# Moving half of a three-term sum from VectorE to GpSimd in an edge pass of a graph network

## The chip, the cores and the metric

The kernel runs on one core of one Trainium2 chip. The metric is the device time of one execution in microseconds (us). The kernel before was timed three times: 6016.84, 6020.4 and 6021.12 us, median 6020.4. One further execution was recorded by the profiler.

## The reference, cut to what matters

The whole kernel applies four graph layers to 6250 nodes with 256 features. The change touches only the edge pass of layer 0. Its 106250 edges are sorted by destination. For each edge the reference computes

```
g0 = f0[edge_src]                      # 64 scalars of the source node
g1 = f1[edge_src]                      # 64 vectors of 3
y0 = edge_attr[:, 0]; y1 = edge_attr[:, 1:4]
m0a = wa * g0 * y0[:, None]
m0b = wb * einsum('eum,em->eu', g1, y1) / sqrt(3)      # a dot product of 3 terms
m1a = wc[:, :, None] * g0[:, :, None] * y1[:, None, :]
m1b = wd[:, :, None] * g1 * y0[:, None, None]
```

where wa, wb, wc and wd come from a small network on the ten further features of the edge. The messages (512 numbers an edge) are summed over the edges of each destination node. The dot product in m0b needs three products, which are formed one by one, and two additions. The change is about these two additions.

## The kernel before, in words

The edges lie in 880 steps of 128 edges, one edge in each partition. Four steps make a group q, and there are 220 groups (NQ). Each engine runs its own program, a loop over periods p = -3 to 221, and in each period every engine works on a group at a different depth of the pipeline. Order between the engines is kept by semaphores, written out by hand; there is no scheduler. In a wait such as `freed(act, s_v, 2 * q - 2)` the engine waits until the semaphore has reached the value, and values of zero or less are not waited for.

- **GpSimd** (L1421) gathers, for each step k, 128 rows of 256 numbers out of the table in HBM by an indirect DMA into one of 8 buffers of G. Before gather k it waits (s_y) until ScalarE has used up the buffer, that is until step k - 8 is done.
- **ScalarE** (`vectors`, L1442 and L1445) scales each gathered row by the four edge attributes: four activations a step. Seven of the message slots go to the tile zt, in one of three sets (z), and the three products of the dot product go to one of two sets t in the same tile. Its first activation of group q waits until the additions of group q - 2 have read set t (s_v). `silu` (L1430) forms the hidden layer of the edge network, once a group, between the second and third step.
- **TensorE** computes the edge weights into PSUM (pE, `edge_weights`, L1548), the hidden layer (pH, L1541), and scatters the messages: `scatter` (L1557) multiplies the 128 x 128 matrix `one` (which edge belongs to which node) with the 512 numbers of a step into pM, one of two PSUM buffers. The first scatter of a group waits for `pair` of that group.
- **VectorE** has the most to do. In period p it issues, in this order: `mark(p)` (L1482, builds `one` for group p out of the PSUM copy pI and relS), `add(p-2, 3)` (L1518, adds pM into the accumulator of a node tile), `dots(p)` (L1489 and L1491, the two additions of the dot product, both with two inputs in SBUF; the second waits for the first), `add(p-1, 0)`, `three(p, 1, 2)` (L1497, three slots times the edge weight), `add(p-1, 1)`, `three(p, 5, 3)` (L1497), `add(p-1, 2)`, `pair(p)` (L1503, the last two slots times their weights). The products read pE from PSUM and zt from SBUF, the adds read acc from SBUF and pM from PSUM.
- Every `add` waits for its scatter (s_m) and for the add before it (s_acc). Every 16 steps, that is once in four periods, `add(p-1, 0)` first loads 16 node numbers into VectorE's registers (L1509).
- **SyncE** loads the edge features and clears the accumulator.

Of the kernel before, what the change touches and what calls it, by code (L numbers as in the profile page):

```python
# [25 lines left out]
K = U2 * math.ceil((ET + math.ceil(N / P) - 1) / U2)  # L26
# [11 lines left out]
def build(nc, a, out):  # L38
# [5 lines left out]
    ALU = mybir.AluOpType  # L44
# [4 lines left out]
    def dram(name, shape, dt=F32):  # L49
        return nc.dram_tensor(name, shape, dt).ap()  # L50
# [55 lines left out]
    table = [dram(f"table{n}", [NP, w]) for n, w in enumerate((D, D + H1, D, D + H3))]  # L106
# [6 lines left out]
    with top:  # L113
# [6 lines left out]
        srcI = top.sb("srcI", [P, KP], I32)  # L120
# [35 lines left out]
        def freed(eng, sem, value):  # L156

            if not (type(value) is int and value <= 0):
                eng.wait_ge(sem, value)
# [577 lines left out]
        def tile(t, n):  # L737

            return t[:, ds(n, 1), :].rearrange("p a c -> p (a c)")
# [187 lines left out]
        with Stage() as st0:  # L927
# [5 lines left out]
            with Stage() as st:  # L933
# [4 lines left out]
                with Stage() as sx:  # L938
# [31 lines left out]
                    s_v, s_tk, s_nd, s_ndd, s_ndr, s_w1, s_w2 = (sx.sem(n) for n in ("s_v", "s_tk", "s_nd", "s_ndd", "s_ndr", "s_w1", "s_w2"))  # L970
# [385 lines left out]
            with Stage() as st:  # L1356
                acc = st.sb("acc0", [P, NT, 2 * D])
                with Stage() as se:
                    NQ, GS, NZ = K // 4, 8, 3
                    G = se.sb("G", [P, GS, D])  # L1360
# [12 lines left out]
                    pM = [se.ps(f"pM{j}", [P, 2 * D]) for j in range(2)]  # L1373
                    pI = se.ps("pI", [P, P])
                    s_w, s_z, s_c, s_i, s_y, s_v, s_p = (se.sem(n) for n in ("s_w", "s_z", "s_c", "s_i", "s_y", "s_v", "s_p"))
                    s_h, s_hs, s_e, s_one, s_m, s_acc = (se.sem(n) for n in ("s_h", "s_hs", "s_e", "s_one", "s_m", "s_acc"))
                    s_g = [se.sem(f"s_g{j}") for j in range(GS)]
                    s_a = [se.sem(f"s_a{j}") for j in range(2)]
                    CLEAR = 4
# [3 lines left out]
                    def z_of(q):  # L1383

                        return zt[:, q % NZ * 32:q % NZ * 32 + 32, :].rearrange("p (s b) c -> p s b c", s=4)

                    def t_of(q):
                        at = NZ * 32 + q % 2 * 12
                        return zt[:, at:at + 12, :].rearrange("p (s m) c -> p s m c", s=4)

                    def periods(do):
                        for p in range(-3, NQ + 2):
                            do(p)

                    with nc.Block() as block:
# [20 lines left out]

                        @block.gpsimd
                        def _(pool):
                            for k in range(K):
                                freed(pool, s_y, k - GS + 1)  # L1420
                                pool.indirect_dma_start(G[:, k % GS, :], None, table[0],  # L1421
                                                        bass.IndirectOffsetOnAxis(ap=srcI[:, k:k + 1], axis=0)).then_inc(s_g[k % GS], 16)

                        @block.scalar
                        def _(act):
                            def silu(q):
                                if 0 <= q < NQ:
                                    act.wait_ge(s_h, q + 1)
                                    freed(act, s_e, 4 * q - 4)
                                    nc.scalar.activation(hid[q % 2][:, :, :], pH[:, :, :], ACT.Silu, scale=1 / math.sqrt(NBAS)).then_inc(s_hs, 1)  # L1430

                            def vectors(q, s):
                                if 0 <= q < NQ:
                                    k = 4 * q + s
                                    act.wait_ge(s_g[k % GS], 16 * (k // GS) + 16)
                                    freed(act, s_m, k - 4 * NZ + 1)
                                    if s == 0:
                                        freed(act, s_v, 2 * q - 2)
                                    g = G[:, k % GS, :].rearrange("p (b c) -> p b c", c=MUL)
                                    zi = q % NZ * 32 + s * 8  # L1440
                                    ti = NZ * 32 + q % 2 * 12 + s * 3
                                    nc.scalar.activation(zt[:, zi:zi + 4, :], g, ACT.Copy, scale=a4S[:, 0, k:k + 1])  # L1442
                                    for m in range(3):
                                        to = slice(zi + 5 + m, ti + m + 1, ti - zi - 5)
                                        ins = nc.scalar.activation(zt[:, to, :], g[:, 0:m + 2:m + 1, :], ACT.Copy, scale=a4S[:, 1 + m, k:k + 1])  # L1445
                                    ins.then_inc(s_y, 1)

                            def period(p):
                                vectors(p + 1, 0)
                                vectors(p + 1, 1)  # L1450
                                silu(p + 2)
                                vectors(p + 1, 2)
                                vectors(p + 1, 3)
                            periods(period)

                        @block.vector
                        def _(dve):
# [26 lines left out]

                            def dots(q):
                                if 0 <= q < NQ:
                                    dve.wait_ge(s_y, 4 * q + 4)
                                    z, t = z_of(q), t_of(q)
                                    nc.vector.tensor_tensor(z[:, :, 4, :], t[:, :, 0, :], t[:, :, 1, :], ALU.add).then_inc(s_v, 1)  # L1489
                                    dve.wait_ge(s_v, 2 * q + 1)  # L1490
                                    nc.vector.tensor_tensor(z[:, :, 4, :], z[:, :, 4, :], t[:, :, 2, :], ALU.add).then_inc(s_v, 1)  # L1491

                            def three(q, b, w):
                                if 0 <= q < NQ:
                                    dve.wait_ge(s_e, 4 * q + 4)
                                    z = z_of(q)[:, :, b:b + 3, :]
                                    nc.vector.tensor_tensor(z, pE[q % 2][:, :, w, :].unsqueeze(2).broadcast_to([P, 4, 3, MUL]), z, ALU.mult)  # L1497

                            def pair(q):
                                if 0 <= q < NQ:  # L1500
                                    dve.wait_ge(s_v, 2 * q + 2)
                                    z = z_of(q)[:, :, 0:5:4, :]
                                    nc.vector.tensor_tensor(z, pE[q % 2][:, :, 0:2, :], z, ALU.mult).then_inc(s_p, 1)  # L1503

                            def add(q, s):
                                k = 4 * q + s
                                if 0 <= q < NQ:
                                    if k % 16 == 0:
                                        _, values = nc.values_load_multi_w_load_instructions(  # L1509
                                            nodeA[0:1, ds(k, 16)], engines=[dve.engine], min_val=0, max_val=NT - 1,  # L1510
                                            skip_runtime_bounds_check_because="the setup clamps every step's node to the node tiles")
                                        at.update(enumerate(values))
                                    if k % 2 == 0 and k // 2 in s_clear:
                                        dve.wait_ge(s_clear[k // 2], 16)
                                    dve.wait_ge(s_m, k + 1)
                                    freed(dve, s_acc, k)
                                    to = tile(acc, at[k % 16])
                                    nc.vector.tensor_tensor(to, to, pM[k % 2][:, :], ALU.add).then_inc(s_acc, 1)  # L1518

                            def period(p):  # L1520
                                mark(p)
                                add(p - 2, 3)
                                dots(p)
                                add(p - 1, 0)
                                three(p, 1, 2)
                                add(p - 1, 1)
                                three(p, 5, 3)
                                add(p - 1, 2)
                                pair(p)
# [252 lines left out]
        with Stage() as st3:  # L1782
# [22 lines left out]
            with Stage() as st:  # L1805
# [9 lines left out]
                s_w, s_c, s_at, s_t, s_tc, s_o, s_r, s_y, s_yb, s_l = (  # L1815
                    st.sem(n) for n in ("s_w", "s_c", "s_at", "s_t", "s_tc", "s_o", "s_r", "s_y", "s_yb", "s_l"))
                s_x = [st.sem(f"s_x{q}") for q in range(5)]
                s_v = [st.sem(f"s_v{j}") for j in range(4)]
# [90 lines left out]
            with Stage() as st:  # L1909
# [8 lines left out]
                s_l, s_h, s_t, s_tc, s_f, s_fc, s_o, s_r = (st.sem(n) for n in ("s_l", "s_h", "s_t", "s_tc", "s_f", "s_fc", "s_o", "s_r"))  # L1918
# [66 lines left out]
            with Stage() as st:  # L1985
                CH = NT // 5
                s_m, s_x, s_out = st.sem("s_m"), [st.sem(f"s_x{q}") for q in range(5)], st.sem("s_out")
# [50 lines left out]
```

## Time and profile before

| | |
|---|---|
| median of three runs | 6020.4 us |
| the profiled execution | 6016.6 us |
| its span (first to last instruction) | 6014.9 us |
| VectorE busy over the span | 4179.2 us (69%) |
| GpSimd busy over the span | 3617.6 us (60%) |
| ScalarE busy over the span | 2463.8 us (41%) |
| TensorE busy over the span | 4348.8 us (72%) |
| layer 0's edge pass | about 285 us to 1706 us of the span |

The shares of the whole span are means over stages with different limits, and for a change in one stage only the rows of that stage count. A row of a timeline gives the start, the length, the engine, the line, the operation and its tiles; neighbours of one kind are merged, with their number behind an x, and in brackets stands how long the engine sat idle before and what ended that. The records of two neighbouring VectorE instructions overlap by some 0.08 us, so the cost of one instruction in a full queue is the distance between two starts and not its own length.

### The profile page before, as it was taken

What the parts mean: (1) busy time and instruction counts of PE and PEld (TensorE: products, weight loads), DVE (VectorE), ACT (ScalarE), POOL (GpSimd) and SP (SyncE); (2) the same over time, 40 slices, a digit from 0 to 9 for tenths busy, and PEclk for the clock granted to TensorE, in tenths of its full rate; (3) what the DMA queues carried; (4) which work ended last, traced back from release to release, by engine and by line L of the source; (5) the groups of instructions that cost most, each with busy time, mean ns of one, the idle gap of its engine ahead of it and who ended that gap; (6) DMA issues with size and microseconds to landing.
All of it is one profiled execution on the core that took longest, in us unless ns stands there. A gap on an engine that the chain in (4) does not pass through costs nothing. (4 is left out here: it accounts for less than half of the span.)

```text
span 6014.9 us, 78255 instructions
## 1 busy us (share of the span) xinstructions
PE 4348.8 (72%) x17463; PEld 2676.3 (44%) x17463; DVE 4179.2 (69%) x9983; ACT 2463.8 (41%) x6920; POOL 3617.6 (60%) x4190
## 2 busy tenths in 40 slices
PE   2799999999995665566567777777856666666596
PEld 1544444444474444444343433344434444444385
DVE  5599999999975556555555555555657766776766
ACT  2498888988853333333320000000113333333343
POOL 3465555555526777777567777777357777775001
PEclk9899999999987777777777677777877777777898
DMA  6453333333335555555333333333235555553301
GB/s 166 162 160 98 98 98 98 97 99 97 98 106 148 140 143 145 141 141 144 110 98 105 105 106 105 105 105 105 95 106 147 148 144 146 147 147 106 100 0 44
DMA packets 468850, 699.69 MB, mean 116 GB/s; under 512 B 212924, under 2 KB 310800, under 8 KB 468262
## 3 DMA queue, kind: packets, MB, share of 16 engines
q0 software_dynamic: 171200, 474.81, 28.4%
q1 hardware_dynamic: 284336, 207.07, 11.9%
q10 hardware_dynamic: 12896, 13.11, 0.6%
q8 instruction: 157, 2.57, 0.2%
q14 instruction: 261, 2.14, 0.1%
HBM read 620.77 MB, written 70.10 MB: 115 GB/s over the span
## 5 line engine op out<-in xcount | busy, mean ns | idle before, releaser
L275 POOL DMA_INDIRECT G<-table,srcI x1760 | 1673.6, 951 | 582.7 <-issue 497.9
L544 PE MATMUL pS<-G,one 128*128 128x260 f32 (+1 forms) x3520 | 1203.6, 480 | 192.2 <-issue 96.2
L1421 POOL DMA_INDIRECT G<-table,srcI x880 | 830.1, 943 | 600.1 <-ACT zt L1445 545.3
L1557 PE MATMUL pM<-zt,one 128*128 128x512 f32 x1760 | 945.2, 618 | 113.3 <-DVE zt L1503 73.7
L477 ACT ACTIVATE acc<-pS x1760 | 691.7, 393 | 779.3 <-PE pS L544 519.5
L625 POOL DMA_INDIRECT G<-table,srcI x880 | 833.5, 947 | 280.9 <-issue 149.0
L661 PE MATMUL pM<-G,one 128*128 128x256 f32 x1760 | 790.5, 555 | 254.7 <-issue 132.5
L1445 ACT ACTIVATE zt<-G,a4S 128x128 f32<-128x128 f32 x2640 | 856.9, 390 | 0.0
L544 PEld LDWEIGHTS pS<-G,one 128*128 128x128 f32 x3520 | 593.0, 212 | 263.3 <-issue 210.1
L661 PEld LDWEIGHTS pM<-G,one 128*128 128x128 f32 x1760 | 374.0, 255 | 657.5 <-DVE one L634 515.3
L641 DVE TENSOR_TENSOR acc<-acc,pM 128x256 f32 x880 | 370.4, 421 | 393.4 <-PE pM L661 388.6
L1518 DVE TENSOR_TENSOR acc<-acc,pM 128x512 f32 x880 | 598.5, 680 | 52.5 <-PE pM L1557 52.5
L429 DVE TENSOR_TENSOR G<-G,pX 128x256 f32<-128x256 f32 (+1 forms) x1320 | 584.8, 504 | 0.0
L850 ACT ACTIVATE y<-acc,shift,rstd 128x256 f32<-128x256 f32 x150 | 88.2, 589 | 1144.7 <-POOL shift L830 1139.7
L345 DVE TENSOR_REDUCE self_s<-pD 128x64 f32<-128x192 f32 (+1 forms) x138 | 47.2, 392 | 707.9 <-DMA G<-table,srcI 707.9
L1548 PE MATMUL pE<-w2s,hid 100*128 100x256 f32 x1760 | 527.7, 381 | 0.0
L1548 PEld LDWEIGHTS pE<-w2s,hid 100*128 100x128 f32 x1760 | 337.3, 192 | 420.8 <-issue 368.6
L1442 ACT ACTIVATE zt<-G,a4S 128x256 f32<-128x256 f32 x880 | 437.4, 497 | 0.0
L1557 PEld LDWEIGHTS pM<-zt,one 128*128 128x128 f32 x1760 | 283.0, 188 | 330.4 <-issue 170.1
L1497 DVE TENSOR_TENSOR zt<-pE,zt 128x768 f32<-128x768 f32 x440 | 418.5, 951 | 0.0
L634 DVE TENSOR_SCALAR one<-iota,relS,wS 128x128 f32<-128x128 f32 x880 | 313.9, 357 | 44.7 <-PE pM L661 34.7
L533 PE MATMUL pD<-parts,oneT 128*128 x1760 | 284.5, 176 | 50.9 <-DVE oneT L332 35.6
(326 smaller groups left out, 5907.1 us busy)
## 6 DMA issues: line engine op xcount, KB each, us to landing
G<-table,srcI POOLq DMA_INDIRECT x3520, 2.8
relT<-step_rel SPq DMA_DIRECT2D x220, 256.0 KB
a10T<-step_a SPq DMA_DIRECT2D x660, 30.0 KB
far<-step_rec SPq DMA_DIRECT2D x224, 64.0 KB
table<-row SPq DMA_DIRECT2D x100, 128.0 KB, 1.7
acc<-zero SPq DMA_DIRECT2D x21, 512.0 KB, 5.1
step_a<-part SPq DMA_DIRECT2D x7, 960.0 KB
table<-row SPq DMA_DIRECT2D x50, 132.0 KB, 1.7
```

The source lines that it names most:

```text
L275: pool.indirect_dma_start(G[:, par * C + j, 0:ROW], None, tab, bass.IndirectOffsetOnAxis(ap=srcI[:, k:k + 1], axis=0)).then_inc(s_g[par * ...
L429: ins = nc.vector.tensor_tensor(z, z, w.unsqueeze(3).broadcast_to([P, 2, 4, F]), ALU.mult)
L477: nc.scalar.activation(tile(whole, to[j]), sum_of(of[j]), ACT.Copy).then_inc(s_out, 1)
L544: nc.tensor.matmul(sum_of(of[j]), one[:, par * C + j, :], G[:, par * C + j, :], start=False, stop=True, skip_group_check=True).then_inc(s_ ...
L625: pool.indirect_dma_start(G[k % u][:, :], None, rows, bass.IndirectOffsetOnAxis(ap=srcI[:, k:k + 1], axis=0)).then_inc(s_g[k % u], 16)
L661: nc.tensor.matmul(pM[j % R][:, :], one[j % R][:, :], G[j][:, :], start=True, stop=True).then_inc(s_m, 1)
L1421: pool.indirect_dma_start(G[:, k % GS, :], None, table[0], bass.IndirectOffsetOnAxis(ap=srcI[:, k:k + 1], axis=0)).then_inc(s_g[k % GS], 16)
L1442: nc.scalar.activation(zt[:, zi:zi + 4, :], g, ACT.Copy, scale=a4S[:, 0, k:k + 1])
L1445: ins = nc.scalar.activation(zt[:, to, :], g[:, 0:m + 2:m + 1, :], ACT.Copy, scale=a4S[:, 1 + m, k:k + 1])
L1518: nc.vector.tensor_tensor(to, to, pM[k % 2][:, :], ALU.add).then_inc(s_acc, 1)
L1548: nc.tensor.matmul(pE[q % 2][:, s, :, :], hid[q % 2][:, s, :], w2s[:, :], start=True, stop=True).then_inc(s_e, 1)
L1557: nc.tensor.matmul(pM[k % 2][:, :], one[q % 2][:, s, :], z_of(q)[:, s, :, :], start=True, stop=True).then_inc(s_m, 1)
```

## The change

- GpSimd makes the first addition, t0 + t1 into slot 4 of z, for group q right behind gather k = 4q + 11. It waits for s_y >= 4q + 4, and raises a new semaphore s_two. Its loop runs on for 8 turns behind the last gather, for the last two groups.
- VectorE makes only the second addition. It waits for s_two in place of s_y, raises s_v once a group (twice before), and is moved in the period from behind `add(p-2, 3)` to behind `add(p-1, 1)`.
- ScalarE waits for s_v >= q - 1 where it waited for 2q - 2, which is the same event: the second addition of group q - 2.
- `three` takes over the wait for s_y, `pair` waits for s_v >= q + 1.

```diff
+                            def two(q):
+                                pool.wait_ge(s_y, 4 * q + 4)
+                                z, t = z_of(q), t_of(q)
+                                pool.tensor_tensor(z[:, :, 4, :], t[:, :, 0, :], t[:, :, 1, :], ALU.add).then_inc(s_two, 1)
+
+                            for k in range(K + GS):
+                                if k < K:
+                                    freed(pool, s_y, k - GS + 1)
+                                    pool.indirect_dma_start(G[:, k % GS, :], ...
+                                if k >= GS and k % 4 == 3:
+                                    two(k // 4 - 2)
...
-                                        freed(act, s_v, 2 * q - 2)
+                                        freed(act, s_v, q - 1)
...
                             def dots(q):
                                 if 0 <= q < NQ:
-                                    dve.wait_ge(s_y, 4 * q + 4)
+                                    dve.wait_ge(s_two, q + 1)
                                     z, t = z_of(q), t_of(q)
-                                    nc.vector.tensor_tensor(z[:, :, 4, :], t[:, :, 0, :], t[:, :, 1, :], ALU.add).then_inc(s_v, 1)
-                                    dve.wait_ge(s_v, 2 * q + 1)
                                     nc.vector.tensor_tensor(z[:, :, 4, :], z[:, :, 4, :], t[:, :, 2, :], ALU.add).then_inc(s_v, 1)
...
                             def three(q, b, w):
                                     dve.wait_ge(s_e, 4 * q + 4)
+                                    dve.wait_ge(s_y, 4 * q + 4)
...
                             def period(p):
                                 mark(p)
                                 add(p - 2, 3)
-                                dots(p)
                                 add(p - 1, 0)
                                 three(p, 1, 2)
                                 add(p - 1, 1)
+                                dots(p)
                                 three(p, 5, 3)
                                 add(p - 1, 2)
                                 pair(p)
```

## Rows read from the trace of the kernel before

**Rows 1.** Windows, one stretch: bounds, length, busy PE, PEld, DVE, ACT, POOL; then the clock.

```profile
500.00:800.00 300.00, 275.75 (x803) 138.00 (x803) 287.43 (x473) 268.24 (x802) 176.87 (x189) 1.00 0.35 98
```

**Rows 2.** Timeline of VectorE, one period, and the same pair of additions a period later.

```profile
1000.96 0.68 DVE L1503 TENSOR_TENSOR zt<-pE,zt 128x512 f32<-128x512 f32 x1
1001.56 0.68 DVE L1482 TENSOR_TENSOR one<-pI,relS 128x512 f32<-128x512 f32 x1
1002.16 0.68 DVE L1518 TENSOR_TENSOR acc<-acc,pM 128x512 f32 x1
1002.75 0.42 DVE L1489 TENSOR_TENSOR zt<-zt 128x256 f32<-128x256 f32 x1
1003.20 0.42 DVE L1491 TENSOR_TENSOR zt<-zt 128x256 f32<-128x256 f32 x1
1003.55 0.68 DVE L1518 TENSOR_TENSOR acc<-acc,pM 128x512 f32 x1
1004.14 0.95 DVE L1497 TENSOR_TENSOR zt<-pE,zt 128x768 f32<-128x768 f32 x1
...
1008.86 0.42 DVE L1489 TENSOR_TENSOR zt<-zt 128x256 f32<-128x256 f32 x1
```

**Rows 3.** The same view, a period in which the registers are loaded.

```profile
1019.29 0.69 DVE L1503 TENSOR_TENSOR zt<-pE,zt 128x512 f32<-128x512 f32 x1
...
1021.54 0.42 DVE L1491 TENSOR_TENSOR zt<-zt 128x256 f32<-128x256 f32 x1
1022.88 0.69 DVE L1518 TENSOR_TENSOR acc<-acc,pM 128x512 f32 x1 [0.91 <-PE pM L1557]
...
1026.41 0.68 DVE L1503 TENSOR_TENSOR zt<-pE,zt 128x512 f32<-128x512 f32 x1
```

**Rows 4.** Line L1509, the register load: whole span, then 1000 to 1032 us.

```profile
L1509 DVEq TENSOR_LOAD <-nodeA x55: 1096/1099/1551, 308.0 to 1683.4; - x55
...
L1509 DVEq TENSOR_LOAD <-nodeA x1: 1097/1097/1097, 1021.6 to 1021.6; - x1
```

**Rows 5.** Line L1518 in 1000 to 1001.5 us: register arithmetic of VectorE's sequencer (DVEq).

```profile
L1518 DVEq FUSED_REGOPS  x1: 57/57/57, 1001.1 to 1001.1; - x1
```

**Rows 6.** Timeline of TensorE in the period of Rows 2.

```profile
1001.74 1.10 PE L1557 MATMUL pM<-zt,one 128*128 128x512 f32 x2 [0.33 <-DVE zt L1503]
...
1007.14 0.38 PE L1541 MATMUL pH<-a10T,w 96*100 96x512 bf16 x1
```

**Rows 7.** Timeline of the pass's last scatters and adds, where nothing lies between them.

```profile
1701.22 4.01 PE L1557 MATMUL pM<-zt,one 128*128 128x512 f32 x8 [0.98 <-DVE zt L1503]
...
1702.46 0.69 DVE L1518 TENSOR_TENSOR acc<-acc,pM 128x512 f32 x1 [0.75 <-PE pM L1557]
...
1703.36 0.69 DVE L1518 TENSOR_TENSOR acc<-acc,pM 128x512 f32 x1 [0.21 <-PE pM L1557]
```

**Rows 8.** Timeline of ScalarE: silu of two neighbouring groups, early; and one step.

```profile
309.94 0.57 ACT L1430 ACTIVATE hid<-pH 100x512 f32<-100x512 f32 x1
...
315.52 0.58 ACT L1430 ACTIVATE hid<-pH 100x512 f32<-100x512 f32 x1
...
1004.49 0.49 ACT L1442 ACTIVATE zt<-G,a4S 128x256 f32<-128x256 f32 x1
```

**Rows 9.** Gathers on GpSimd: timeline early and in mid pass; then line L1421's landing.

```profile
292.95 0.95 POOL L1421 DMA_INDIRECT G<-table,srcI  x1 [0.30 <-issue]
...
1004.86 0.94 POOL L1421 DMA_INDIRECT G<-table,srcI  x1 [0.33 <-ACT zt L1445]
...
DMA to landing us min/median/max: 2.6/2.8/6.5
```

**Rows 10.** Line L1737 (layer 1's nodes): min/median/max ns, first and last start.

```profile
L1737 POOL TENSOR_TENSOR acc<-acc,xr x50: 719/726/911, 3000.1 to 3105.4; 128x256 f32<-128x256 f32 x50
```

**Rows 11.** Timeline 3000.9 to 3001.5 us, both engines adding at once.

```profile
3000.18 1.81 DVE L1732 TENSOR_TENSOR acc<-acc,den 128x256 f32<-128x256 f32 x2
...
3000.80 0.90 POOL L1737 TENSOR_TENSOR acc<-acc,xr 128x256 f32<-128x256 f32 x1
```

More of the change, by code:

```diff
@@ L1375, in build @@
                     s_w, s_z, s_c, s_i, s_y, s_v, s_p = (se.sem(n) for n in ("s_w", "s_z", "s_c", "s_i", "s_y", "s_v", "s_p"))
-                    s_h, s_hs, s_e, s_one, s_m, s_acc = (se.sem(n) for n in ("s_h", "s_hs", "s_e", "s_one", "s_m", "s_acc"))
+                    s_h, s_hs, s_e, s_one, s_m, s_acc, s_two = (se.sem(n) for n in ("s_h", "s_hs", "s_e", "s_one", "s_m", "s_acc", "s_two"))
                     s_g = [se.sem(f"s_g{j}") for j in range(GS)]
@@ L1418, in _ @@
                         def _(pool):
[L1419 to L1422, printed above, removed]
+                            def two(q):
[5 more added lines that the diff above has]
+                                    freed(pool, s_y, k - GS + 1)
+                                    pool.indirect_dma_start(G[:, k % GS, :], None, table[0],
+                                                            bass.IndirectOffsetOnAxis(ap=srcI[:, k:k + 1], axis=0)).then_inc(s_g[k % GS], 16)
+                                if k >= GS and k % 4 == 3:
+                                    two(k // 4 - 2)
                         @block.scalar
@@ L1500, in pair @@
                                 if 0 <= q < NQ:
-                                    dve.wait_ge(s_v, 2 * q + 2)
+                                    dve.wait_ge(s_v, q + 1)
                                     z = z_of(q)[:, :, 0:5:4, :]
```

## The prediction

> **What bounds the kernel now.** I read the busy time in stretches first. Between 500 and 800 us VectorE is busy 287.43 of 300 us, TensorE 275.75, ScalarE 268.24, GpSimd 176.87 [rows 1]. So in this pass VectorE is the fullest, TensorE and ScalarE are close behind, and GpSimd has room. The granted clock is 1.00, the upper level of 2.4 GHz, so no clock effect is in play.
>
> Second, VectorE's timeline, by starts. From pair to pair (L1503) an ordinary period takes 6.11 us, as from L1489 at 1002.75 to L1489 at 1008.86 [rows 2]: ten instructions without a hole. Once in four periods it takes 7.12 us, from 1019.29 to 1026.41 [rows 3]. The whole difference lies between the second addition at 1021.54 and the next add at 1022.88, 1.34 us where an ordinary period has 0.35. The row names a scatter, but that scatter was done long before. What fills the gap is the register load of 1.10 us that starts at 1021.6 [rows 3, 4]. There are 55 such loads [rows 4]. Of the 220 groups I leave out the first three and the first load, in which the pass gets going: 163 periods of 6.11 and 54 of 7.12 remain, mean 6.36.
>
> So VectorE's own queue sets the end, and a dearer thing than the addition stands in it: a load behind an instruction on which the queue is held.
>
> **Removed from VectorE.** The first addition costs from its start to that of the second, 1003.20 - 1002.75 = 0.45 us, more than its 0.42 us of length, as the second waits for it and the sequencer with it. The second costs 1003.55 - 1003.20 = 0.35 us and stays, at another place [rows 2]. If nothing else became late, an ordinary period would take 6.11 - 0.45 = 5.66 us.
>
> **What is late next: the first add.** Count from the start T of a pair. Before, mark comes at T + 0.60, add(p-2, 3) at T + 1.20, the two additions, and add(p-1, 0) at T + 2.59 [rows 2]. Now nothing lies between the two adds, and the queue could take the second at T + 1.79. Two things forbid it. It needs its scatter: this starts at T + 0.78 (1001.74 against 1000.96) and at the end of the pass an add starts 1.24 us behind the start of its scatter (1702.46 against 1701.22), so T + 2.02 [rows 2, 6, 7]. And it waits for the add before: adds with nothing between them start 0.90 us apart (1703.36 - 1702.46) where they could be 0.60 apart [rows 2, 7]. That gives T + 1.20 + 0.90 = T + 2.10, the later of the two. The two additions had covered this, so 0.31 us of the 0.45 comes back as a wait. An ordinary period takes 5.66 + 0.31 = 5.97 us, less by rounding: I take 5.96.
>
> **The register load.** It is the larger term. VectorE's sequencer runs ahead of the engine: the register arithmetic for the add that starts at 1002.16 is done at 1001.1, while pair is executing and mark waits [rows 2, 5]. Before, it could not be ahead at the load, because the second addition is held until the first is done; the load begins within 0.1 us of it and the add 1.34 us behind it [rows 3, 4]. In the changed order no held addition stands ahead of the load. It would begin near T + 0.2, right behind the arithmetic of add(p-2, 3), and end near T + 1.3, and with the 0.22 us that lie between its end and the add (1022.88 less 1021.56 + 1.10) it is ready by T + 1.6, ahead of T + 2.10: hidden. Bounds: at best it costs nothing; at worst it begins only when add(p-2, 3) itself starts, T + 1.20, and the add comes at T + 2.52, 0.42 later, so 6.39 us in one period of four. I take nothing, because the row of register arithmetic shows the sequencer that far ahead; neither end relies on the queue being deeper than the two entries seen.
>
> **The moved addition.** Behind add(p-1, 1) it costs the same 0.35 us, which is within the 5.66. It waits for s_two. `three` waits for s_y as well, an event long past: ScalarE ends the group at 1004.49 + 0.10, and the additions come at 1008.86 [rows 2, 8].
>
> **GpSimd.** Back to back a gather takes 0.95 us with 0.30 idle ahead of it, 5.0 us for four [rows 9]. The added addition is not in the trace, but one of the same size is: 128x256 f32 with two SBUF inputs takes 0.726 us, 0.719 to 0.911 [rows 10]. What lies around it is open. Below: gap 0.03 us ahead, and the 0.30 us ahead of each gather counted once as now, so 5.8 us a period. Above: a further 0.30 us of idle, as ahead of each gather, and the longest addition, 0.91: 6.2 us. I take 5.8, since a wait of 0.33 us ahead of a gather even where ScalarE is late by little [rows 9] says that the gap belongs to gathers. Then GpSimd is just under 5.96. Its s_y wait for group q is the one that gather 4q + 11 has just passed, so it adds no wait. Queued behind it are the next gathers, which are now up to 0.8 us later; their data has 8 buffers, some 10 us of ScalarE's work, against 0.94 us of issue and 2.8 us to landing, so nobody waits.
>
> **ScalarE.** Its bare group takes 315.52 - 309.94 = 5.58 us [rows 8], under 5.96. Its release by the second addition moves from T + 2.66 (1003.62) to T + 4.57; before, it started the next group 0.9 us behind that release (1004.49), now it will wait for it, 0.38 us a group (5.96 - 5.58) [rows 2, 8]. This doesn't close a tight loop: from that release, 5.6 us of ScalarE, 1.3 us of gather and 0.8 us of addition, 7.7 us, stand against two periods, 11.9 us, before VectorE needs the sum.
>
> **TensorE** ends its period's work with pH at T + 6.18 + 0.38 (1007.14 against 1000.96) [rows 6], its waits among it (0.33 us ahead of the first scatter); the next scatter is due at 5.96 + 0.78 = T + 6.74. It fits.
>
> **Start.** The first sum now needs one more gather (1.25) and the addition (0.73) behind ScalarE, 2 us; half of it is covered by the product put ahead of it on VectorE. I take +1 us, between 0 and 2.
>
> **Sum.** 163 x (6.11 - 5.96) = 24 us, 54 x (7.12 - 5.96) = 63 us, less 1 us: 86 us. The profiled execution took 6016.6 us, which gives 5930.6; the median of the runs lies 3.8 us above it, so 5934 us.
>
> **Two rules of the Trainium skill.** A GpSimd addition of 128x256 takes 0.726 us where VectorE's takes 0.42 [rows 2, 10]. The Trainium skill (GPSIMD Engine Reference, Engine selection) says that elementwise work with two inputs belongs on VectorE, as GpSimd is about twice as slow. The ratio here is 1.7, so the trace agrees nearly; by that rule the change loses 0.3 us of work a group, which matters only if GpSimd becomes the bound. The other is a rival below.
>
> **Rivals.**
> A. GpSimd becomes the bound at 6.05 to 6.2 us. For: 5.0 + 0.73 + 0.30 is already 6.03. Against: the row of the gathers puts the gap ahead of a gather. At 6.05: 217 x (6.36 - 6.05) = 67 us, 5953; at 6.2: 35 us, 5986.
> B. The load is hidden only in part, 6.39 us in each fourth: 54 x 0.43 = 23 us given back, 5957.
> C. The lock, the way to slower. Where both engines add from two SBUF inputs at once, VectorE's 0.42 us becomes some 0.94 (two in 1.81 us, overlapping a little) and GpSimd's 0.73 becomes 0.90 [rows 2, 10, 11]. If the second addition met GpSimd's in every period, a period would take 5.96 + 0.52 = 6.48, 217 x 0.12 = 26 us slower, 6046; it decides once 0.40/0.52, 77% of the groups, meet. Against: VectorE's addition lies behind add, product and add, T + 2.10 + 0.59 + 0.87 + 0.59 = T + 4.15, to T + 4.57 (0.59 is the start-to-start of the add and 0.87 that of the product, its 0.95 less the overlap of 0.08), and GpSimd's follows ScalarE's last step by about 1.25 us, which is near T + 5.6 to T + 6.3. The Trainium skill (SBUF — State Buffer, SBUF: two separate sides) states it as an exclusive lock, held for the whole instruction, between a GpSimd operation and a VectorE one with two SBUF inputs; the trace agrees with its 0.90. Products and adds here have one input in PSUM and show no such stretch.
> D. ScalarE's later release makes it the bound and nothing is gained: the pass would stay near 6.36 and the time near 6020. Against: 4 us of room.
>
> **Chances.** Forecast 0.52, rival A 0.17, B 0.17, C 0.06, D 0.04, and 0.04 that the period falls below 5.96 (scatter only: 5.89, 15 us less, 5919). The range runs from 5915 to 5985, which takes in A nearly to its upper bound. A measurement here tells about 0.2% (12 us) from no change. Faster: forecast, A, B, the low case and a rest, 0.90; same 0.04; slower 0.06.
>
> **What would show it.** Pair to pair 5.96 in all periods, with no longer fourth. L1518 behind L1518 0.90 apart, named as waiting for the scatter. The load starting some 2 us ahead of its add. GpSimd's addition near 0.73 us and the gather behind it 0.3 later. ScalarE waiting for the second addition once a group. Wrong would be: periods of 6.05 or more with GpSimd never idle (A), a fourth period of 6.4 (B), the VectorE addition at 0.9 us (C), or VectorE idle ahead of it (D).

## The result, and the profile after

The changed kernel takes 5925.8 us (median of 4 runs, 5923.85 to 5932.97) against 6018.6 us for the kernel before (4 runs, 6010.4 to 6021.12). The ratio is 0.985, with a 95% interval of 0.9833 to 0.9867: 93 us faster. The forecast was 5934 us, with a range of 5915 to 5985. The profiled execution took 5923.9 us, its span is 5922.2 us.

The row below answers to [rows 1]: the same stretch, the same columns.

```profile
500.00:800.00 300.00, 283.10 (x856) 154.12 (x855) 289.06 (x454) 286.57 (x857) 228.98 (x253) 1.00 0.38 104
```

VectorE is as busy as before (289.06 against 287.43 us). It executes 454 instructions and not 473, though it gets through more groups, because a group now takes nine of them and not ten. GpSimd has gone from 176.87 to 228.98 us. TensorE executes 856 instructions and not 803, ScalarE 857 and not 802, 7% more each in the same time.

VectorE's timeline (start, length, line, operation). The line numbers have moved: pair is L1510, mark L1490, the adds L1525, the products L1504, the remaining addition L1497. It answers to [rows 2]:

```profile
1001.13 0.68 DVE L1510 TENSOR_TENSOR zt<-pE,zt 128x512 f32<-128x512 f32 x1
1001.73 0.68 DVE L1490 TENSOR_TENSOR one<-pI,relS 128x512 f32<-128x512 f32 x1
1002.33 0.68 DVE L1525 TENSOR_TENSOR acc<-acc,pM 128x512 f32 x1
1003.22 0.69 DVE L1525 TENSOR_TENSOR acc<-acc,pM 128x512 f32 x1 [0.21 <-PE pM L1564]
1003.82 0.95 DVE L1504 TENSOR_TENSOR zt<-pE,zt 128x768 f32<-128x768 f32 x1
1004.69 0.68 DVE L1525 TENSOR_TENSOR acc<-acc,pM 128x512 f32 x1
1005.28 0.42 DVE L1497 TENSOR_TENSOR zt<-zt 128x256 f32<-128x256 f32 x1
1005.62 0.95 DVE L1504 TENSOR_TENSOR zt<-pE,zt 128x768 f32<-128x768 f32 x1
...
1007.08 0.68 DVE L1510 TENSOR_TENSOR zt<-pE,zt 128x512 f32<-128x512 f32 x1
```

From pair to pair it is 5.95 us. The second add starts 0.89 us behind the first and shows 0.21 us of idle time ahead of it. A period with a register load answers to [rows 3, 4]; the load is L1516:

```profile
1018.99 0.68 DVE L1510 TENSOR_TENSOR zt<-pE,zt 128x512 f32<-128x512 f32 x1
...
1020.19 0.68 DVE L1525 TENSOR_TENSOR acc<-acc,pM 128x512 f32 x1
1021.07 0.69 DVE L1525 TENSOR_TENSOR acc<-acc,pM 128x512 f32 x1 [0.21 <-PE pM L1564]
...
1024.94 0.69 DVE L1510 TENSOR_TENSOR zt<-pE,zt 128x512 f32<-128x512 f32 x1
```

```profile
L1516 DVEq TENSOR_LOAD <-nodeA x1: 1101/1101/1101, 1019.3 to 1019.3; - x1
```

This period is 5.95 us long too. The load begins 0.3 us behind the start of pair and is over before the first of the two adds ends. GpSimd's timeline answers to [rows 9, 10], with the addition in L1422 and the gather in L1427:

```profile
1006.11 0.94 POOL L1427 DMA_INDIRECT G<-table,srcI  x1 [0.33 <-ACT zt L1453]
1007.08 0.74 POOL L1422 TENSOR_TENSOR zt<-zt 128x256 f32<-128x256 f32 x1
1007.97 0.96 POOL L1427 DMA_INDIRECT G<-table,srcI  x1 [0.16 <-issue]
1009.24 0.95 POOL L1427 DMA_INDIRECT G<-table,srcI  x1 [0.30 <-issue]
```

The addition starts 0.03 us behind the end of the gather, takes 0.74 us, and 0.16 us later the next gather starts. Last, two groups of waits of the changed kernel between 500 and 1590 us (who waited for whom; total us, times, longest):

```profile
ACT zt L1450 <- DVE zt L1497: 48.9, 180, 0.6
DVE acc L1525 <- PE pM L1564: 39.8, 183, 0.6
```

Where the time came from. The lines of the pass's adds (min/median/max ns, first and last start), before and after:

```profile
L1518 DVE TENSOR_TENSOR acc<-acc,pM x880: 673/680/690, 309.7 to 1705.4; 128x512 f32 x176
```

```profile
L1525 DVE TENSOR_TENSOR acc<-acc,pM x880: 669/678/690, 305.7 to 1614.3; 128x512 f32 x176
```

Between the first and the last add it was 1395.7 us and is 1308.6, so the pass gave 87.1 us of the 92.7 between the spans. Of the rest, 4.0 us lies ahead of the pass (its first add starts at 305.7 and not 309.7) and 1.6 us behind it, in stages the change doesn't touch.

### The profile page after: what moved, and what is told of

It reads as the page before. It is cut to its first block and busy times, and to the rows that moved or that the text cites. A ratio compares the mean times of both kernels' runs of the same rounds, so it can differ in the third digit from the quotient of the medians.

```text
span 5922.2 us, 78695 instructions
## 1 busy us (share of the span) xinstructions
PE 4287.7 (72%) x17463; PEld 2697.7 (46%) x17463; DVE 4098.9 (69%) x9763; ACT 2463.1 (42%) x6920; POOL 3788.9 (64%) x4410
## 5 line engine op out<-in xcount | busy, mean ns | idle before, releaser
L1427 POOL DMA_INDIRECT G<-table,srcI x880 | 837.4, 952 | 338.4 <-ACT zt L1453 190.1
L1564 PE MATMUL pM<-zt,one 128*128 128x512 f32 x1760 | 916.5, 601 | 74.7 <-DVE zt L1510 74.1
L1525 DVE TENSOR_TENSOR acc<-acc,pM 128x512 f32 x880 | 598.1, 680 | 52.1 <-PE pM L1564 52.1
L1504 DVE TENSOR_TENSOR zt<-pE,zt 128x768 f32<-128x768 f32 x440 | 418.2, 950 | 8.1 <-PE pE L1555 8.1
L1564 PEld LDWEIGHTS pM<-zt,one 128*128 128x128 f32 x1760 | 314.5, 189 | 212.2 <-issue 170.7
L551 PE MATMUL pS<-nought 128*128 128x1 bf16 x1762 | 306.4, 174 | 18.6 <-DVE parts L320 18.6
```

Source lines behind the costliest of these rows:

```text
L1427: pool.indirect_dma_start(G[:, k % GS, :], None, table[0], bass.IndirectOffsetOnAxis(ap=srcI[:, k:k + 1], axis=0)).then_inc(s_g[k % GS], 16)
L1564: nc.tensor.matmul(pM[k % 2][:, :], one[q % 2][:, s, :], z_of(q)[:, s, :, :], start=True, stop=True).then_inc(s_m, 1)
```

## The experiments

The kernel before was timed beside each of these kernels; its median was 6018.8 us beside e1 to e4, 6021.0 beside e5 to e8, 6023.7 beside e9, and the ratios are against that. Periods are measured from mark to mark in each trace; what is said of "all periods" leaves out the first few and the last, and a few in mid pass that are up to 0.4 us longer.

**e1: the second addition stays where it was.** Against the changed kernel:

```diff
                                 add(p - 2, 3)
+                                dots(p)
                                 add(p - 1, 0)
                                 three(p, 1, 2)
                                 add(p - 1, 1)
-                                dots(p)
```

> As the changed kernel (GpSimd makes the first addition), but VectorE's second addition stays where it was, between add(p-2, 3) and add(p-1, 0). Theory of the held queue: the saving comes from taking the first addition and the hold out, not from the move, and the second addition covers the 0.31 us that two adds in a row lose. Then an ordinary period is 6.11 - 0.45 = 5.66 to 5.70 us, the load stays hidden, and the time is 217 x 0.27 = 59 us below the changed kernel, near 5867 us. Rival, the move is needed: in the old place the second addition waits for GpSimd's, or the load is late again; then the fourth period stays near 6.6 or all periods near 5.95, and the time is 5910 or more. Rival, GpSimd's floor: four gathers and an addition take 5.67 us in the changed kernel's trace, so it could show as 5.70 to 5.75.

Measured: 5872.6 us, ratio 0.9761 (0.9745 to 0.9777), 53 us faster than the changed kernel. VectorE's timeline of it:

```profile
1001.77 0.69 DVE L1510 TENSOR_TENSOR zt<-pE,zt 128x512 f32<-128x512 f32 x1
...
1002.97 0.69 DVE L1525 TENSOR_TENSOR acc<-acc,pM 128x512 f32 x1
1003.56 0.43 DVE L1497 TENSOR_TENSOR zt<-zt 128x256 f32<-128x256 f32 x1
1003.89 0.69 DVE L1525 TENSOR_TENSOR acc<-acc,pM 128x512 f32 x1
...
1007.42 0.69 DVE L1510 TENSOR_TENSOR zt<-pE,zt 128x512 f32<-128x512 f32 x1
```

The two adds are now 0.92 us apart with the addition between them, and the period is 5.65 us. The addition costs almost nothing there (0.03 us), since the adds would be 0.89 apart anyway. So the split makes the gain, and the move gives 0.30 us a period back. This version beats both kernels.

Of the 54 periods with a load behind the first, 50 take 5.65 to 6.02 us, most of them 5.65: there the load stays hidden, or nearly so. The other four are 6.65 to 6.81 us long. One of them:

```profile
604.31 0.75 POOL L1422 TENSOR_TENSOR zt<-zt 128x256 f32<-128x256 f32 x1
604.36 0.68 DVE L1525 TENSOR_TENSOR acc<-acc,pM 128x512 f32 x1
605.09 0.43 DVE L1497 TENSOR_TENSOR zt<-zt 128x256 f32<-128x256 f32 x1
606.43 0.69 DVE L1525 TENSOR_TENSOR acc<-acc,pM 128x512 f32 x1 [0.91 <-PE pM L1564]
```

```profile
L1516 DVEq TENSOR_LOAD <-nodeA x1: 1101/1101/1101, 605.1 to 605.1; - x1
```

Here GpSimd's addition ends at 605.06, later than in most periods, and VectorE's waits for it until 605.09. The load stands behind that wait, begins at 605.1 and leaves VectorE idle for 0.91 us. It is the held load again, now held by the other engine. In all four periods VectorE's addition starts within 0.05 us of the end of GpSimd's, where the median over the pass is 1.15 us.

**e2: the move alone.** The kernel before with the same lines moved, both additions still on VectorE, and `three` waiting for s_y.

> As the kernel before, both additions on VectorE, but both moved behind add(p-1, 1). Theory: the load no longer has a held instruction ahead of it and is hidden, while the two adds in a row lose 0.31 us in every period: 6.11 + 0.31 = 6.42 us in all periods, against a mean of 6.36, so 10 to 15 us slower than before, near 6032 us. Rival, the load is not hidden by the absence of a held instruction: 6.42 in three and 7.1 or more in the fourth period, 40 us slower or more. Rival, the move alone makes the gain: 5.95 to 6.1.

Measured: 6027.4 us, ratio 1.0016 (1.0006 to 1.0026). Nearly all periods are 6.41 or 6.42 us, the longest 6.76, none 7.1. A period with a load:

```profile
1026.58 0.68 DVE L1519 TENSOR_TENSOR acc<-acc,pM 128x512 f32 x1
1027.47 0.69 DVE L1519 TENSOR_TENSOR acc<-acc,pM 128x512 f32 x1 [0.21 <-PE pM L1558]
```

```profile
L1510 DVEq TENSOR_LOAD <-nodeA x1: 1102/1102/1102, 1025.7 to 1025.7; - x1
```

The load is hidden even with both additions on VectorE, once neither stands ahead of it; the price is the wait between the adds, in every period. The two nearly cancel: 8.6 us slower, where 10 to 15 were expected.

**e3: the load alone.** The kernel before with the register load ahead of the additions:

```diff
                                 add(p - 2, 3)
+                                nodes(p - 1)      # the load, taken out of add(p - 1, 0)
                                 dots(p)
                                 add(p - 1, 0)
```

> The kernel before with one edit: the load of 16 node numbers is issued ahead of the two additions (behind add(p-2, 3)) and not behind them. Theory: the sequencer is then some 1 us ahead of the engine, the load runs beside pair, mark and the add, and the fourth period falls from 7.12 to 6.11: 54 x 1.01 = 55 us faster than before, near 5964 us, with the first addition still on VectorE. Rival, a load holds the engine wherever it stands: no change, 6018.

Measured: 5957.3 us, ratio 0.99 (0.9883 to 0.9916), 61 us faster than the kernel before. All periods are 6.11 or 6.12 us. A period with a load:

```profile
1017.75 0.68 DVE L1503 TENSOR_TENSOR zt<-pE,zt 128x512 f32<-128x512 f32 x1
...
1019.99 0.42 DVE L1491 TENSOR_TENSOR zt<-zt 128x256 f32<-128x256 f32 x1
1020.33 0.68 DVE L1521 TENSOR_TENSOR acc<-acc,pM 128x512 f32 x1
```

```profile
L1508 DVEq TENSOR_LOAD <-nodeA x1: 1096/1096/1096, 1018.1 to 1018.1; - x1
```

The load now begins 1.9 us ahead of the second addition, and the 1.34 us between that addition and the next add are 0.34. Its profiled execution took 5975.2 us, 18 more than its median, but its pass, from first gather to last add, is 54.6 us shorter than the one before (1365.5 against 1420.1), which is the 55 expected. Moving one load ahead of the two additions is worth two thirds of the whole change.

**e4: no first addition at all.** The changed kernel, where GpSimd adds nothing and VectorE adds t1 and t2 behind a wait for s_y. The first product is missing from the sum.

> The changed kernel without the first addition on any engine (VectorE adds two of the three products, the first product is left out of the sum); VectorE waits for ScalarE directly. Theory: GpSimd's addition costs nothing where it stands, periods stay 5.95 and the time within 5 us of the changed kernel's 5926. Rival A or C (GpSimd's work or the lock takes part in the bound): the periods fall below 5.95, to 5.89 or lower, 13 us or more faster.

Measured: 5931.0 us, ratio 0.9853 (0.9837 to 0.987), not to be told from the changed kernel. Periods stay 5.95. GpSimd's addition costs nothing that this can show in the changed kernel.

**e5: e1 without the first addition.** The first product is missing here too.

> The version in which VectorE's second addition stays in its old place (e1), without the first addition on any engine (the first product is left out of the sum). In e1 a period takes 5.65 us on VectorE and also on GpSimd, which never waits. If VectorE's queue is the bound (6.11 - 0.45 = 5.66), nothing changes: 5.65 us, 5865 to 5875 us in all. If GpSimd's floor is the bound, the periods fall below 5.65, toward ScalarE's 5.58, and the time to 5860 or less.

Measured: 5871.1 us, ratio 0.9755 (0.9738 to 0.9771), not to be told from e1. GpSimd waits again for ScalarE ahead of its gathers, and the period is still 5.65: VectorE's queue is the bound of e1, if only just, as GpSimd in e1 waits for nothing but its own issue:

```profile
1005.11 0.94 POOL L1427 DMA_INDIRECT G<-table,srcI  x1 [0.30 <-issue]
1006.35 0.94 POOL L1427 DMA_INDIRECT G<-table,srcI  x1 [0.30 <-issue]
1007.31 0.74 POOL L1422 TENSOR_TENSOR zt<-zt 128x256 f32<-128x256 f32 x1
1008.21 0.97 POOL L1427 DMA_INDIRECT G<-table,srcI  x1 [0.16 <-issue]
```

(That is e1.) Its four gathers and one addition fill 5.65 us as well (1007.31 less the addition at 1001.66). That leaves it no room to catch up when it is late, and e1's four long periods, which e5 hasn't, are the price. They cost some 4.5 us. The profiled pass of e1, from first gather to last add, is 8.6 us longer than that of e5 (1277.0 against 1268.4), though the medians are only 1.5 us apart.

**e6: both additions on GpSimd.**

```diff
 pool.tensor_tensor(z[:, :, 4, :], t[:, :, 0, :], t[:, :, 1, :], ALU.add).then_inc(s_one2, 1)
+pool.wait_ge(s_one2, q + 1)
+pool.tensor_tensor(z[:, :, 4, :], z[:, :, 4, :], t[:, :, 2, :], ALU.add).then_inc(s_v, 1)
```

> The changed kernel with both additions on GpSimd, one behind the other, and none on VectorE. VectorE alone would need 5.95 - 0.34 = 5.61 us. Theory (rival A's mechanism, GpSimd's time simply adds up): the floor of 5.65 us for four gathers and one addition rises by 0.74 and a gap of 0.05 to 0.1, to 6.45 us in all periods, 217 x 0.08 = 18 us slower than before, near 6036 us. Rival, GpSimd has hidden room or the buffers absorb it: 5.95 or less. If the additions of both engines' port met, their records would be longer than 0.75 us.

Measured: 6032.0 us, ratio 1.0018 (1.0009 to 1.0028); all periods 6.42 or 6.43. VectorE now waits for GpSimd once a group:

```profile
1001.66 0.69 DVE L1510 TENSOR_TENSOR zt<-pE,zt 128x512 f32<-128x512 f32 x1 [0.72 <-POOL zt L1424]
```

So GpSimd has room for one addition and not for two. This is rival A, reached at the second addition.

**e7: no GpSimd, the two additions apart.** As e3, with the first addition ahead of mark and the second behind the load.

> No GpSimd: both additions on VectorE, the first moved ahead of mark, so that the second no longer waits in the queue behind it, and the load issued ahead of the second. Theory: the hold is gone, each addition costs 0.35 us, so 6.11 - 0.45 + 0.35 = 6.01 us in all periods, no longer fourth: 217 x 0.35 = 76 us faster than before, near 5942 us, 16 us slower than the changed kernel. Rival, the load is late because more instructions stand in the queue ahead of it: fourth periods of 6.4 or more.

Measured: 5939.2 us, ratio 0.9868 (0.9852 to 0.9885); all periods 5.99. Its interval overlaps that of the changed kernel, so the two are not told apart. 82 us of saving need no GpSimd, only that nothing is issued straight behind what it waits for, and that the load stands early.

**e8: the load behind a wait again.** The changed kernel with one wait moved:

```diff
+                                    freed(dve, s_acc, k)
                                     if k % 16 == 0:
                                         ...
-                                    freed(dve, s_acc, k)
```

> The changed kernel with the wait for the add before (s_acc) put ahead of the register load and not behind it. Nothing else changes. Theory: the sequencer then stands until add(p-2, 3) has ended, T + 1.92, and the load of 1.10 us and 0.2 us behind it come on top: the add comes at T + 3.2 and not T + 2.1, a fourth period of 7.05 to 7.1 us beside 5.95, 55 x 1.1 = 61 us slower than the changed kernel, near 5987 us. Rival, the load is cheap wherever it stands: 5926 us.

Measured: 6010.6 us, ratio 0.9981 (0.9972 to 0.9991), 24 us more than expected. Its timeline in a period with a load:

```profile
1015.05 0.68 DVE L1525 TENSOR_TENSOR acc<-acc,pM 128x512 f32 x1
1017.02 0.69 DVE L1525 TENSOR_TENSOR acc<-acc,pM 128x512 f32 x1 [1.29 <-issue]
1017.62 0.95 DVE L1504 TENSOR_TENSOR zt<-pE,zt 128x768 f32<-128x768 f32 x1
1018.49 0.68 DVE L1525 TENSOR_TENSOR acc<-acc,pM 128x512 f32 x1
1019.08 0.82 DVE L1497 TENSOR_TENSOR zt<-zt 128x256 f32<-128x256 f32 x1
1019.83 0.94 DVE L1504 TENSOR_TENSOR zt<-pE,zt 128x768 f32<-128x768 f32 x1
```

and GpSimd's beside it:

```profile
1018.55 0.95 POOL L1427 DMA_INDIRECT G<-table,srcI  x1 [0.33 <-ACT zt L1453]
1019.52 0.97 POOL L1422 TENSOR_TENSOR zt<-zt 128x256 f32<-128x256 f32 x1
```

The load (L1517) now begins at 1015.8, as the first add ends, and costs what was expected: the adds are 1.97 us apart and not 0.89, 1.08 more. But such a period is 7.44 us long and not 7.03. The other 0.41 is in VectorE's addition, which takes 0.75 us to the next start and not 0.34, while GpSimd's is stretched to 0.97. The late load has moved the two additions onto each other. Of the 54 periods with a load 46 are some 7.44 us long, and in 44 of these VectorE's addition takes 0.74 us or more; the other eight are 7.03, and in them it takes 0.42.

**e9: e8 without GpSimd's addition.** The first product is missing from the sum.

> e8 without the first addition on any engine (the first product is left out of the sum). In e8 the period with a load took 7.44 us, of which the held load explains 1.08 (7.03), and VectorE's addition is 0.82 us long in it and not 0.42, with GpSimd's addition, 0.97 us long, beside it. Theory (the two additions meet, and each stretches the other): with GpSimd's addition gone VectorE's is 0.42 us long everywhere, the period with a load falls to 7.03 and the time by 54 x 0.41 = 22 us, from 6010 to about 5988. Rival, the stretch comes from the gather or from the held load itself: 7.44 stays, and 6010.

Measured: 5996.4 us, ratio 0.9955 (0.9939 to 0.9972). The pass, first gather to last add, takes 1393.3 us against 1412.4 in e8, 19 us less, where 22 were expected; between the medians it is 14. Nearly all periods with a load are 7.03 or 7.04. The line of VectorE's addition in e8, then in e9 (min/median/max ns):

```profile
L1497 DVE TENSOR_TENSOR zt<-zt x220: 415/418/879, 302.1 to 1688.5; 128x256 f32<-128x256 f32 x110
```

```profile
L1497 DVE TENSOR_TENSOR zt<-zt x220: 414/418/441, 303.0 to 1671.0; 128x256 f32<-128x256 f32 x110
```

No addition longer than 0.44 us is left. GpSimd's gathers are still there and GpSimd's additions are not, so it is the additions that stretch VectorE's. That is rival C's stretch, shown in this pass.

## Why the prediction was right

**Removed and kept.** The first addition was put at 0.45 us of queue and the floor of the period at 5.66 us. e1 has 5.65.

**Two adds in a row.** Forecast 0.90 us apart, a wait of 0.31; measured 0.89 and, as e1 has no such wait, 0.30 a period. The end of the pass in the trace before [rows 7] had shown the case. The profile names the scatter in this gap (39.8 us in all), but the scatter starts at 1001.92, T + 0.79, and would allow the add at T + 2.03; it starts at T + 2.09, which is where the wait for the add before puts it. The scatter, on TensorE:

```profile
1001.92 1.10 PE L1564 MATMUL pM<-zt,one 128*128 128x512 f32 x2 [0.33 <-DVE zt L1510]
```

VectorE's sequencer has one wait (L159, at 1003.0, as the first add ends) and then the register arithmetic of the second add (L1525, at 1003.1) in this gap, which fits. But no run took that wait away by itself, and the scatter comes so close behind it that, by the same bound, only 0.06 us of the 0.30 would be given back.

**The register load.** The largest term, 63 us with its share of the ordinary saving, came as worked out: the load runs beside pair and mark, and the fourth period is like the others, so rival B fell. e3 has it alone (55 us of the pass), e2 shows that the move by itself hides it, e8 that one wait ahead of it brings it back. The four long periods of e1 show the same with a wait for another engine. What hid it was not GpSimd and not the removal of work but the absence of a held instruction in front.

**The sum.** 24 + 63 - 1 = 86 us was forecast, 87.1 measured in the pass. The two periods alone would give 89 us (163 x 0.16 and 54 x 1.17); three periods of 6.3 us and a last one of 6.42 take 1.6 us back. The start term was mis-sized: the first add stands 24.4 us behind the first gather in both traces (24.42 before, 24.35 after), so it was 0 and not 1 us. The remaining difference to 93 us lies outside the pass, where two executions of unchanged stages differed by 5.6 us.

**GpSimd.** 5.8 us was taken as its floor, between 5.8 and 6.2. It is 5.65: the addition starts 0.03 us behind a gather and the gather behind it comes after 0.16 us, so the addition replaces part of a gap that gathers show among themselves (0.30). Rival A, which needed a further 0.30, is ruled out by e4 and e5, and e6 shows where it begins.

**ScalarE** waits for the second addition as forecast, 48.9 us in 180 groups, 0.27 us a group where 0.38 was worked out. It changes nothing: the period is made up of VectorE's own queue and its wait between the two adds, and between 500 and 1590 us VectorE shows no wait for ScalarE. So rival D fell.

**The lock (rival C)** all but never acts in the changed kernel, as VectorE's addition lies at T + 4.15 and GpSimd's mostly at T + 5.65 (T + 5.95 in the row shown above). One of 220 additions of VectorE is stretched, near the end of the pass, where GpSimd's comes late:

```profile
1600.69 0.72 POOL L1422 TENSOR_TENSOR zt<-zt 128x256 f32<-128x256 f32 x1 [4.74 <-ACT zt L1453]
```

```profile
1600.82 0.88 DVE L1497 TENSOR_TENSOR zt<-zt 128x256 f32<-128x256 f32 x1
```

Its price was put at 0.52 us a meeting; in e8 it is 0.41. The Trainium skill (SBUF — State Buffer, SBUF: two separate sides) has the one who starts first go on undisturbed and the other block. The two rows above agree: GpSimd's addition starts 0.13 us ahead and keeps its 0.72 us, VectorE's takes 0.88. In the meetings of e8 VectorE's starts first, 0.44 us ahead of GpSimd's recorded start, and there the records differ from that rule: VectorE's is stretched to 0.82 all the same, and GpSimd's to 0.97. GpSimd's records are rough in such a profile, so the form stays open; that the two disturb each other doesn't.

**What the forecast did not see** is that the change contains a step against itself. It said that 0.31 of the 0.45 us comes back as a wait, but did not ask what the addition would cover if it stayed. That is 0.30 us a period, 65 us over 217 periods. e1 measured 53 us: its four exposed loads take back 4.5 us, and its first add comes 3.4 us later behind the first gather (27.7 against 24.4 us). The profiled pass is 56 us shorter.

## What to carry to other kernels

A queue that is full is not yet a queue of useful work: find what stands in it behind an instruction that waits for its neighbour (here a register load of 1.1 us), since moving that alone may be worth most of what taking work away gives (e3: 61 us for one moved load, of 93). Two dependent instructions with nothing between them lose time here, 0.30 us for the adds of 128x512 and 0.10 for the additions of 128x256 (0.45 against 0.35), and a short one in that gap that neither waits for is almost free (0.03 us in e1); so before moving an instruction ask what it covers where it stands. Work can be given to a second engine as long as its own queue has room, and that room is read from its back-to-back instructions, not from its busy share (one addition free in the changed kernel, the second 0.47 us a period in e6). A wait on that second engine then stands in the first one's queue, so keep what must be early ahead of it (e1's four long periods).

## What the runs showed of the hardware that was not expected

- A gather is itself stretched where VectorE adds from two SBUF inputs at its start: 1.15 us instead of 0.94 in e2, with the two additions at 1003.88 and 1004.34. In e2 199 of 880 gathers take over 1.0 us, and all but the very first start while such an addition runs; 224 others overlap such an addition elsewhere, or by less than their first 0.2 us, and take no longer than 1.0.

```profile
1004.43 1.15 POOL L1421 DMA_INDIRECT G<-table,srcI  x1 [0.33 <-ACT zt L1445]
```

  In e7 the longest takes 1.24 us. No period of e7 is longer for it: they are all 5.99.
- The gap ahead of a gather is 0.30 us behind another gather and 0.16 us behind an addition of GpSimd.
- Delaying one engine by 1.08 us in one period of four cost 1.49 us, because it moved the additions of two engines onto each other (e8, e9). In the changed kernel GpSimd's addition starts 0.8 us or more behind the end of VectorE's in mid pass.
